# Two spare matmuls in each of the last 16 attention steps, and a reciprocal moved from step 8 to step 16

## The reference

```
x = x + attn(layernorm(x))
x = x + ffn(layernorm(x))

attn: q, k, v = projections;  scores = q k^T / 4;  softmax over the keys;  (attn v) w_o^T
ffn:  xq = int4_quant(x);  gate, up = xq @ ternary weights;  inter = int8_quant(up * relu(gate)^2)
      out = inter @ ternary(w_down)
```

## Time and profile before

| | |
|---|---|
| median of 3 runs | 1107.39 us (1103.1 to 1108.71) |
| the profiled execution's own time | 1107.77 us |
| its span, first to last instruction | 1106.0 us |
| mean granted TensorE clock | 0.946 of full |
| PE busy | 993.5 us, 90% of the span |
| DVE busy | 862.5 us, 78% |
| ACT busy | 779.8 us, 71% |

### The profile page before, as it was taken

One profiled execution on the slowest core, in us unless ns is written; L12 is line 12 of the kernel. 1 busy time (PEld: TensorE's weight loads), 2 busy tenths in 40 slices (PEclk: granted clock), 3 DMA queues, 4 the chain that ended last, 5 costly groups with the idle time before them and its releaser, 6 DMA issues.

```text
span 1106.0 us, 16495 instructions
## 1 busy us (share of the span) xinstructions
PE 993.5 (90%) x5789; PEld 278.5 (25%) x5806; DVE 862.5 (78%) x1544; ACT 779.8 (71%) x1404; POOL 139.8 (13%) x285
## 2 busy tenths in 40 slices
PE   5478999999999999999999999998878979999997
PEld 3122222222222222222221222221111114444443
DVE  6187579888889888988889888999963227878874
ACT  5344248888888888888888888888858525766665
POOL 3400000110102101111012010110000011112110
PEclk9879899999999999999999999999978568999999
DMA  9510011102101111111110210211453023111001
GB/s 358 177 51 1 1 29 34 35 26 71 40 21 48 48 41 49 35 41 46 51 35 20 63 54 20 50 44 35 133 189 87 9 91 91 48 39 57 21 20 39
DMA packets 37993, 64.90 MB, mean 59 GB/s; under 512 B 3606, under 2 KB 18966, under 8 KB 37654
## 3 DMA queue, kind: packets, MB, share of 16 engines
q1 hardware_dynamic: 37910, 63.85, 19.4%
HBM read 42.27 MB, written 21.23 MB: 57 GB/s over the span
## 4 chain that ended last, share of the span: by engine, by line
PE 67%; DVE 12%; ACT 10%; issue 7%; DMA 2%; SPq 1%; POOL 0%; ACTq 0%; POOLq 0%; DVEq 0%
PE ps L422 18%; PE ps L365 15%; DVE mx L930 9%; PE ps L401 8%; PE ps L343 8%; PE ps L463 5%; PE ps L307 5%; PE ps L486 4%; PE ps L510 3%; ACT PB L660 2%; ACT OS L666 1%; ACT nmT L671 1%; ACT PB L738 1%; DMA qk<-att_d 1%; ACT XV L716 1%
## 5 line engine op out<-in xcount | busy, mean ns | idle before, releaser
L930 DVE TENSOR_REDUCE mx<-ps 128x1 f32<-128x512 f32 x1024 | 644.7, 684 | 91.5 <-PE ps L365 91.2
L660 ACT ACTIVATE PB<-ps 128x512 f32<-128x512 f32 x1024 | 560.1, 595 | 146.5 <-PE ps L401 140.3
L365 PE MATMUL ps<-QK 48*128 48x512 f16 x1024 | 304.6, 389 | 34.4 <-DVE mx L930 34.1
L401 PE MATMUL ps<-QK 50*128 50x512 f16 x1024 | 299.8, 396 | 5.7 <-ACT PB L660 4.6
L422 PE MATMUL ps<-PB,Vg 128*32 128x512 f32 x2048 | 287.5, 635 | 0.7 <-ACT PB L660 0.7
L365 PEld LDWEIGHTS ps<-QK 48*128 48x128 f16 x1024 | 77.7, 93 | 392.9 <-DVE mx L930 303.8
L343 PE MATMUL ps<-XV,wqk 128*128 128x512 f16 x384 | 111.7, 387 | 14.1 <-ACT nmT L671 14.1
L1161 POOL TENSOR_SCALAR nmb<-nm 128x16 f16<-128x16 f32 x32 | 6.6, 205 | 630.8 <-DVE nm L935 630.8
L401 PEld LDWEIGHTS ps<-QK 50*128 50x128 f16 x1024 | 58.5, 95 | 43.9 <-ACT PB L660 42.2
L422 PEld LDWEIGHTS ps<-PB,Vg 128*32 128x32 f32 x2048 | 41.0, 110 | 110.7 <-ACT PB L660 95.5
L463 PE MATMUL ps<-wo,XV 128*128 128x512 f32 x128 | 60.2, 614 | 1.6 <-DVE wqk L960 0.9
(11 more groups left out here) (133 smaller groups left out, 652.8 us busy)
## 6 DMA issues: line engine op xcount, KB each, us to landing
parts_d<-spl SPq DMA_DIRECT2D x64, 128.0 KB
att_d<-OS SPq DMA_DIRECT2D x32, 256.0 KB
QK<-parts_d SPq DMA_DIRECT2D x48, 128.0 KB, 4.7
QK<-parts_d SPq DMA_DIRECT2D x16, 256.0 KB, 4.4
wqk<-x SPq DMA_DIRECT2D x16, 256.0 KB, 6.7
XV<-att_d SPq DMA_DIRECT2D x2, 2048.0 KB, 8.5
QK<-rden_d SPq DMA_DIRECT2D x8, 512.0 KB, 7.7
out<-PB SPq DMA_DIRECT2D x16, 256.0 KB, 2.0
```

Source lines behind the costliest of these rows:

```text
L365: nc.tensor.matmul(ps[:, at % S_BANKS, :], QK[rows, sup % 2, 2 * set_ + p, 0, half * HALF + qt * P:half * HALF + (qt + 1) * P], QK[rows, s ...
L401: nc.tensor.matmul(ps[:, T_BANK + n % T_BANKS, :], QK[rows, sup % 2, 2 * set_ + p, 1, kt * P:(kt + 1) * P], QK[rows, sup % 2, 2 * set_ + p ...
L660: nc.scalar.activation(PB[:, at % 3, 2 * (i % 2) + i // 2, :], ps[:, T_BANK + n % T_BANKS, :], ACT.Exp, scale=exp_reg).then_inc(probs, 1)
L930: nc.vector.tensor_reduce(mx[:, v % 2, idx, kh:kh + 1], ps[:, at % S_BANKS, :], AX.X, ALU.max).then_inc(s_used, 1)
```

## The change

In the last superunit each of the steps 16 to 31 gets two more matmuls of 128x128 by 128x512 in bf16. Their operands are the identity and the ternary gate weight, which is in place; they write banks 0 and 1, whose content nobody reads any more, and no engine waits for them. Before the first pair PE waits until the gate weight is ready and until DVE has read the last score bank. The reciprocal of batch 0 moves on DVE's queue from behind the maxima of step 8 to step 16, behind the last maximum.

```
+        def pe_spare(pe, step):
+
+            if step == STEPS - AHEAD:
+                pe.wait_ge(w_tern[0], 4)
+                pe.wait_ge(s_used, SUP_ITEMS * SUPERS)
+            for m in range(2):
+                nc.tensor.matmul(ps[:, m, :], identb[:], tg[:, m, 0:HALF], start=True, stop=True)
...
                 item(step, 3)
                 pe_scoresT(pe, sup, step, 3)
+                if last and step >= STEPS - AHEAD:
+                    pe_spare(pe, step)
                 if r == 1 and at + 1 < UNITS:
                     pe_max_rows(pe, at + 1)
...
-                if last and step == 8:
+                if last and step == 16:
                     dve_reciprocal(dve, 0)
```

## The result

The changed kernel takes 1074.83 us (median of 4 executions, 1070.91 to 1077.07). The kernel before, with a fourth execution added, takes 1106.04 us (1103.1 to 1108.71). The ratio is 0.9715, with a 95% interval of 0.9673 to 0.9756.

The account below looks back on a forecast made before the run. Two separate losses were taken to bound the kernel: the reciprocal's stall at step 8 and PE's halved clock in steps 16 to 31. 10.5 + 18.8 - 1.6 = 27.7 us off 1107.4 gave about 1080 us, range 1074 to 1092.

Parts of the forecast that it names:

- The reciprocal's stall: Steps 8 to 10: moving the reciprocal to step 16 turns 18.60 us into 8.10, a gain of 10.5 us.
- SP's queue: `sp_rden_out` now waits until about 829, but the transfers behind it are due later, so SP loses nothing.
- Steps 17 to 31: Between these steps' value products: 50.97 us becomes 35.0 at full clock, a gain of 16.0 us.
- The last `act_abs`: Within steps 17 to 31: one more `act_abs` of 1.37 us, of which 1.2 us was counted as added time.
- the first output projection: In the tail's start: 5.36 us at low clock against 3.67 for the second at full clock, a gain of 1.7.
- The spares' own cost: Steps 16 to 31: 0 to 0.2 us a step, taken as 0.1, 1.6 us in all; upper bound 3.2.
- the projection pair: Nearest profile row for timing spares: starts 0.31 behind the matmul before; next matmul 0.54 after the pair's start.
- The 0.35 and 0.4: Counted at full clock: 0.35 us for step 20's small fp32 matmul and weight load, 0.4 for step 25's copy.
- the lower bound: Spares cost 0 us a step: score 2 still starts 1.07 us after score 3, sharing the array with score 1.
- the whole return hangs on what the spares add: After step 16: spares raise PE from 70% to 87% busy, so the clock holds; forecast chance 0.72.
- the two gains: 10.5 us from moving the reciprocal and 18.8 us from the returned clock, added together.

Follow-up runs that it names:

- the delay: 128x128 scratch reciprocal on DVE in step 4, added to the reciprocal moved alone (1096.82, 1075.22, 1071.72, 1076.94, 1071.06 us) and the changed kernel (1076.69, 1071.10, 1076.05, 1071.10 us).
- the tail's spares: Changed kernel with 18 more 128x512 spare matmuls behind the second output projection; 1075.69 us (6 executions, 1071.44 to 1081.14).
- narrow spares: Changed kernel with the two spare matmuls cut to 48 of the 128 rows; 1077.2 us in one execution.
- the two executions of one kernel above: Changed kernel with spares only from step 20 on, run twice: 1081.2 us (clock fell, then returned) and 1074.71 us (never fell).

## Why the prediction was right, and what it left out

**The reciprocal's stall: right in place and size.** The three steps took 18.60 us and take 811.21 - 803.09 = 8.12: 10.5 gained, as predicted. It appears alone when the spares are kept: the mean is 1085.2 with the stall and 1074.7 without (14 timed executions of the changed kernel, ten of them with the delay or the tail's spares), 10.5 us; by medians, 1084.1 and 1075.7, it is 8.4. The executions are from several chips, so the last microsecond or two isn't certain. DVE had no wait. SP's queue lost nothing: it sent the reciprocals out at 823.66, and the next transfer, the sums, was due at 827.52 only.

**Steps 17 to 31: right.** Forecast 35.0 us between the products of steps 17 and 31 before the spares' cost, measured 863.43 - 828.84 = 34.6 with spares and 865.39 - 831.26 = 34.1 with the reciprocal moved alone. The last `act_abs` added 0.9 and not 1.2. Behind them, 865.21 - 863.43 = 1.78 (forecast 1.75) and 3.70 for the first output projection (forecast 3.65 or so).

**The spares' own cost: over-sized.** I took 0.1 us a step from the projection pair, 1.6 in all. A plain step measures 2.39 with and without them. Over steps 15 to 31 the ruler has 40.77 with and 40.32 without: 0.45 us. It is all in two steps: 0.11 in step 20, where the small matmul for the mean is, and 0.36 in step 25, where the copy is (2.81 us with spares, 2.45 without). The 0.35 and 0.4 that I counted for these two steps at full clock hardly exist without spares. In a plain step the lower bound was right: score 0 starts 0.85 behind score 3, as forecast, and the three scores take 0.60 together, so score 1 and score 2 do share the array. The four-spare kernel shows where the cover ends.

**The sum of the profiled execution.** The span is 34.5 us shorter. From the ruler: 4.5 before the products of step 8 (807.58 against 803.09; clock in the start, 0.88 against 0.91), 10.5 stall, 57.37 - 40.77 = 16.6, 0.9 behind the last products, 1.65 in the first output projection with its wait, 0.4 elsewhere. Without the start's 4.5 it is 30.0, against 27.7 + 1.6 expected without the spares' cost. The median moved by 31.2 against 27.7 forecast; how much of that is the start's luck isn't known, since one execution of each kernel was profiled.

**The step that was incomplete: "the whole return hangs on what the spares add".** I added the two gains as if the fall after step 16 were certain without spares, and the rows of one execution made it look so. It isn't. With the reciprocal at 16 and no spares, 10 of 15 timed executions took 1071 to 1077 us and 5 took 1091 to 1097, which by their mean clock are those that lost it; the mean of the 15 is 1081.3. With two or more full-row spares in all 16 steps and the reciprocal at 16, none of 15 was above 1081.2 (the highest, 1081.14 at a mean clock of 0.972, was not profiled, so a short fall in it isn't excluded). If spares made no difference, all 5 of the 30 executions that fell would be among the 15 without spares with a chance of 2% (3003/142506). With the reciprocal at step 8, 27 of 29 timed executions of before are at 1098 or above and two at 1085 and 1087; with spares added, none of 10 is above 1091.44. So by the means the spares are worth 1100.3 - 1085.2 = 15 us to the kernel before, but only 1081.3 - 1074.7 = 6.6 us once the reciprocal is moved (an estimate from few executions, good for 1 to 12), and in a median of few executions they may be worth nothing or 16. The mechanism was right, the split between the two edits was not.

**What stays open.** Why the stall at step 8 makes the later fall so much more frequent (27 of 29 against 5 of 15) isn't settled. A guess is that it depends on the time from the clock's return, near 826 in the kernel before, to the steps after 16; the delay was meant to test such a dependence and did not decide it. Nor is it known how few spares, or how narrow, would do: the kernels with one spare and with narrow spares were run once each, in executions that might have kept the clock with none.

The Trainium skill ("TensorE: Matmul & The Clock Gate", on the clock gate) has sustained activity release the throttle. Two executions here speak against taking busy time as that activity: 92% busy at 0.50 for 48 us and for 58 us. With full-row spares added it did come back, in one execution. The same page of the Trainium skill says of a kernel's start that the same kernel leaves the low clock after a different number of matmuls from run to run. Here the clock of the first 170 us does vary, from 0.83 to 0.91, and in the two executions of one kernel above so does a fall in mid kernel.

## What to carry to other kernels

When one profile shows a stretch at half clock, time the kernel many times and look at the mean clock of each execution before crediting an edit: in four executions the reciprocal alone looked as good as the whole change, in the next eleven (five of them with the small delay) it lost the clock five times. Filler matmuls cost little as long as they fit into a wait of TensorE that another engine ends, so measure that wait in the loop (0.47 us here took two, not four). And look for a small instruction on a busy engine's queue that waits for a transfer: 5.8 us of waiting and 1.75 us of the instruction cost 10.5 us, since the clock fell as well.

## What the runs showed of the hardware

The clock in the first 170 us differs between executions with the same work there: 0.83 to 0.91 in the 14 profiles. The products of step 8 came at 812.23 in the one with 0.83, and at 802.23 and 803.09 in the two with 0.91. The times differ too: the changed kernel's four executions lie at 1070.9 and 1073.3 with a mean clock of 0.982 and 0.981, and at 1076.4 and 1077.1 with 0.976. That spread of 6 us is more than the 2 or 3 us that the tail's spares were meant to bring; that it comes from the start is likely by the profiles, but three of these four executions were not profiled.

A busy PE doesn't by itself get the high clock back: it was busy for 92% of 48 us and of 58 us and stayed at 0.50.

Two matmuls of 48 and 50 rows on different sides of the array started 0.01 us apart, while a matmul of all 128 rows started 0.32 us after the 50-row one before it.
